# Cross-attention heads on one core: which maximum tiles stand beside which score chunk

## What is computed

```
q = _qdq(x) @ _qdq(wq).T + bq
kv = cond @ wkv.T + bkv
k, v = jnp.split(kv, 2, axis=-1)
...
attn = jax.nn.softmax(jnp.einsum('bnhd,bmhd->bhnm', q, k) * scale, axis=-1)
o = jnp.einsum('bhnm,bmhd->bnhd', attn, v).reshape(B, N, C)
out = _qdq(o) @ _qdq(wp).T + bp
```

## Time and profile before

| | |
|---|---|
| median of 3 runs | 620.76 us |
| profiled execution, its own time | 621.35 us |
| its span (first to last instruction) | 619.5 us |
| mean granted TensorE clock over the span | 0.989 of full |
| busy: PE, PEld | 594.8, 472.6 us |
| busy: DVE, ACT, POOL | 387.1, 305.4, 226.6 us |
| maximum tiles (line 1321), DVE's reads of them (line 982) | 240 of each |
| DMA of keys for the heads (`k_stack`) | 90 of 256 KB |

### The profile page before, as it was taken

How to read it: one execution, slowest core, us unless ns; L and a number is a source line. 1 busy time by engine, 2 the same in 40 slices (tenths; PEclk the granted TensorE clock), 3 DMA queues, 4 the chain that set the end, 5 groups by cost and what they waited for, 6 DMA issues and landing times. The chain is left out here.

```text
span 619.5 us, 12268 instructions
## 1 busy us (share of the span) xinstructions
PE 594.8 (96%) x4264; PEld 472.6 (76%) x4264; DVE 387.1 (62%) x699; ACT 305.4 (49%) x440; POOL 226.6 (37%) x111
## 2 busy tenths in 40 slices
PE   8989999999999999999999999978799899999997
PEld 7867788888887676666666766655698789799996
DVE  3996531430344898988998989956754244376562
ACT  4544233233233665666655666653248668644441
POOL 0000200000011887888888888860001554400000
PEclk9999999999999999999999999987999899999999
DMA  8873655524549666655666666500041324155410
GB/s 300 297 234 129 183 187 161 203 70 164 205 122 288 151 167 167 165 148 148 151 174 164 166 171 160 144 2 2 1 145 59 136 78 195 69 180 195 173 63 35
DMA packets 29758, 92.19 MB, mean 149 GB/s; under 512 B 5472, under 2 KB 9568, under 8 KB 23008
## 3 DMA queue, kind: packets, MB, share of 16 engines
q1 hardware_dynamic: 28480, 89.67, 48.0%
q10 hardware_dynamic: 1248, 2.10, 0.9%
HBM read 65.02 MB, written 18.35 MB: 135 GB/s over the span
## 5 line engine op out<-in xcount | busy, mean ns | idle before, releaser
L982 DVE TENSOR_REDUCE m_part<-ps 128x1 f32<-128x512 f32 x240 | 152.6, 683 | 18.9 <-PE ps L1321 18.3
L716 ACT ACTIVATE p_ring<-ps 128x1024 f32<-128x1024 f32 x128 | 125.6, 1023 | 68.7 <-PE ps L1431 32.6
L589 POOL TENSOR_TENSOR p_sum<-p_sum,p_ring 128x1024 f32<-128x1024 f32 x45 | 107.1, 2380 | 4.1
L1321 PE MATMUL ps<-k_stack,q_max 96*128 96x512 f32 x240 | 92.3, 432 | 0.5 <-issue 0.3
L1419 PEld LDWEIGHTS ps<-q_stack,k_stack 98*128 98x128 f32 x512 | 77.2, 193 | 12.5 <-ACT p_ring L716 4.1
L1419 PE MATMUL ps<-q_stack,k_stack 98*128 98x256 f32 x512 | 85.3, 291 | 0.0
L1431 PE MATMUL ps<-p_ring,v_head 128*32 128x256 f32 x1024 | 70.1, 389 | 1.9 <-ACT o_t L698 1.7
L1321 PEld LDWEIGHTS ps<-k_stack,q_max 96*128 96x128 f32 x240 | 42.3, 188 | 24.5 <-issue 13.8
L937 DVE SCALAR_TENSOR_TENSOR kl_buf<-ps,biases,kh_buf 128x512 fp32r<-128x512 f32 x32 | 23.6, 747 | 55.9 <-ACT kh_buf L670 55.5
L315 DVE TENSOR_TENSOR l_ring<-f_ring,h_ring 128x2048 fp32r<-128x2048 f32 x22 | 50.2, 2287 | 12.5 <-ACT h_ring L311 12.5
L343 PE MATMUL ps<-xt_h,h_ring 128*128 128x256 f32 x200 | 56.8, 284 | 0.0
(11 more groups left out here) (194 smaller groups left out, 1070.5 us busy)
## 6 DMA issues: line engine op xcount, KB each, us to landing
f_ring<-stream SPq DMA_DIRECT2D x29, 1024.0 KB, 4.9
k_stack<-kh_scratch SPq DMA_DIRECT2D x60, 256.0 KB, 4.5
kh_scratch<-kh_buf SPq DMA_DIRECT2D x32, 256.0 KB, 5.6
kl_scratch<-kl_buf SPq DMA_DIRECT2D x32, 256.0 KB, 5.8
v_head<-v_all SPq DMA_DIRECT2D x16, 512.0 KB, 4.0
k_stack<-kl_scratch SPq DMA_DIRECT2D x30, 256.0 KB, 4.1
v_all<-stream SPq DMA_DIRECT2D x4, 256.0 KB, 4.9
f_ring<-stream SPq DMA_DIRECT2D x4, 256.0 KB, 5.5
```

The costliest lines, as they stand in the source:

```text
L589: nc.gpsimd.tensor_tensor(p_sum[:, p, :], p_ring[:, 0, :] if n == 0 else p_sum[:, p, :], p_pair[:] if c == 3 else p_ring[:, c % 4, :], ALU ...
L716: nc.scalar.activation(p_ring[:, c % 4, :], ps[:, 2 * (c % 2):2 * (c % 2) + 2, :].rearrange("p b n -> p (b n)"), ACT.Exp, scale=XSCALE).th ...
L982: nc.vector.reduce_max(m_part[:, j // NT, j % NT:j % NT + 1], maximum_bank(j), AX.X).then_inc(max_read, 1)
L1321: nc.tensor.matmul(maximum_bank(j), q_max[p][0:SPLIT_ROWS, at128(j % NT)], k_stack[p][0:SPLIT_ROWS, j // NT * D:(j // NT + 1) * D], start= ...
```

## The change

Every head keeps its 8 score chunks, 8 value chunks, 16 tiles, merge and rows. What moves is their order on PE, and on DVE the place of the pair sum and of one tile read:

```diff
             negate_maximum(0)
-            chunk_maxima(1, 0, 3)
+            chunk_maxima(1, 0, 4)
...
                 first = isinstance(h, int) and h == 0
-                chunk_maxima(h + 1, 3, 11)
+                chunk_maxima(h + 1, 4, 12)
                 add_pair(h)
-                chunk_maxima(h + 1, 11, 16)
+                chunk_maxima(h + 1, 12, 16)
                 negate_maximum(h + 1)
                 if after:
                     chunk_maxima(h + 2, 0, 1)
                 if not first:
                     normalize_output(h - 1)
                 if after:
-                    chunk_maxima(h + 2, 1, 3)
+                    chunk_maxima(h + 2, 1, 4)
...
                 score(0)
-                next_maxima(3, 5)
+                next_maxima(4, 5)
                 score(1)
                 next_maxima(5, 7)
                 score(2)
-                next_maxima(7, 8)
+                next_maxima(7, 9)
                 score(3)
-                next_maxima(8, 10)
+                next_maxima(9, 10)
                 if not first:
                     summed_denominators(h - 1, 1 - p)
-                next_maxima(10, 11)
+                next_maxima(10, 12)
                 score(4)
-                next_maxima(11, 12)
+                next_maxima(12, 13)
                 score(5)
-                next_maxima(12, 14)
+                next_maxima(13, 15)
                 for c in range(4):
                     value(c)
-                next_maxima(14, 15)
-                score(6)
                 next_maxima(15, 16)
                 if after_loads is not None:
                     maxima(h + 2, p, after_loads, 0, 1)
-                score(7)
+                score(6)
                 if not first:
                     merge(h - 1)
+                score(7)
                 if after_loads is not None:
                     maxima(h + 2, p, after_loads, 1, 2)
                 for c in range(4, 7):
                     value(c)
                 maximum_rows(h + 1)
                 value(7)
                 if after_loads is not None:
-                    maxima(h + 2, p, after_loads, 2, 3)
+                    maxima(h + 2, p, after_loads, 2, 4)
...
             maximum_rows(0)
             pe.wait_ge(ones_set, 3)
-            maxima(1, 1, 1, 2, 3)
+            maxima(1, 1, 1, 2, 4)
             head(0, 0, 1, 1, 2, first=True)
```

## The result

The changed kernel takes 632.88 us (median of 4 runs, 631.56 to 634.4) against 621.68 us of the kernel before in the same comparison. The ratio is 1.018, with a 95% interval of 1.0138 to 1.0221: slower by 1.4 to 2.2%. The profiled execution took 631.56 us, its span is 629.8 us.

A forecast was written before the change was run, and what follows sets the result against it. Prediction: PE is gated at tile 0 by the landing of the keys; 0.25 + 0.48 less about 0.03 us over 14 heads, 9.8, plus 0.6 in head 15, gives 10.4 us: 631.2 us against the median, range 628.0 to 635.0.

The forecast's parts named there:

- The gate: Tile 0 of the head after next waits for its first half of keys, starting 0.24 and 0.22 us after landing.
- Step 1: Moved tiles 3 and 8 put one more tile ahead of score chunk 3, delaying the key load 0.25 us a head.
- Step 2: Score chunk 6 moves from ahead of tile 0 to behind it, costing 0.48 us a head.
- the slack: Slack that early key landings leave at tile 0: about 0.03 us less loss a head.
- Step 3: Merge moved between score chunks 6 and 7, behind tile 0 before and after: no cost.
- Step 4: DVE's pair sum one read later, so POOL's chain ends 0.6 us later; PE waits 0.6 us once, in head 15.
- The sum: Heads 0 to 13 lose 0.70 us each, 9.8 us; with head 15's 0.6 us, 10.4 us in all.
- The keys are not the gate: Tile 0 does not wait for its keys, so the change is not slower: 620.6 us, or 620.0 against the median; 7%.
- The tile 8 rival: Second half of the keys also gates tile 8: 2.1 us more over 14 heads, 633.3 us; 11%.
- The pairs pay: Tiles in pairs and the moved merge remove PE's short waits: at most 5.6 us faster, 615.2 us; 3%.
- The clock: PE's wait in each head lowers the granted clock to 1.2 GHz for 3 us: 21 us more, 652 us; 2%.

The follow-up runs named there:

- run 1: Changed kernel with the first half of the keys loaded as two quarters, each requested earlier: 620.02 us, ratio 0.9995 against the kernel before.
- run 2: Kernel before with the first half of the keys loaded as two quarters, each requested earlier: 619.0 us, ratio 0.9963.
- run 6: Kernel before with the first half of the keys requested after score chunk 4, not chunk 3: 665.76 us in a single run.
- run 3: Changed kernel with score chunk 6 again ahead of tile 0: 626.28 us, ratio 1.0081 against the kernel before.
- the tiles alone: Changed kernel with score chunk 6 ahead of tile 0 and the merge behind chunk 7, as before: 624.68 us, ratio 1.0064 against the kernel before.
- run 4: Kernel before with score chunk 6 alone moved behind tile 0: 626.15 us, ratio 1.0083.
- merge alone: Kernel before with only the merge moved between score chunks 6 and 7: 621.67 us, ratio 1.0020.
- run 5: Two kernels: the change's moved tiles and pair sum only, 624.68 us, ratio 1.0064; kernel before with only the merge moved, 621.67 us, ratio 1.0020.
- the second kernel of run 7: Changed kernel with early key quarters, pair sum back after tile 10's read, and tile 14 back behind the values: 620.38 us, ratio 0.9998 against the kernel before.
- Run 7: Changed kernel with early key quarters and DVE's pair sum back after tile 10's read: 635.7 us, ratio 1.0241; then tile 14 behind the values: 620.38 us.

## Why the prediction was right, by its own steps

- **The gate.** Right, and shown: with earlier keys both orders run at 14.1 us a head (runs 1, 2), with later ones the head grows by nearly the delay (run 6, heads at full clock: 1.8 to 2.1 us for 2.05).
- **Step 1, one tile more ahead of the request,** 0.25 us a head: 0.24 measured in run 3 and in the SP rows of head 6; 0.16 in the tiles alone without their one odd head.
- **Step 2, chunk 6 behind the gate,** 0.48 us less the slack: 0.45 measured (run 4).
- **Step 3, the merge:** nothing, as forecast (merge alone); beside the moved tiles it isn't settled (run 5).
- **Step 4, POOL's chain,** 0.6 us in head 15: the wait grew by 0.62 us, a closer match than the step deserves. From head 14's first scores POOL's end moved by 0.83 us (16.89 to 17.72); run 1 and the second kernel of run 7, which differ in the places of the pair and of tile 14, give 0.82. The mechanism is right and its size was too small, for a reason left open. 0.22 us of it went into head 14, which became that much longer, and the rest is the wait. Nor did it reach the total. The part from head 15's first scores to its merge became 0.59 us shorter, since the clock, low there in both kernels, came back sooner in this execution (6.8 us at the lower level, 10.2 before); further on it was lower for longer (0.66 in the stretch from 445 to 450 us, 1.00 before). These are single executions, and I can't tell which part of that -0.59 and of the +1.23 behind it belongs to the change.
- **The sum.** 9.8 us were forecast for heads 0 to 13 and 9.76 measured: 0.73 a head in heads 1 to 12 and 0.66 in head 13 for a forecast of 0.70, and 0.40 in head 0. For the profiled execution 631.75 was forecast, and it took 631.56. That these meet within 0.2 us is luck, since the parts that nobody forecast (-0.40 ahead of head 0, -0.59 where +0.6 was expected, +1.23 at the end) happen to cancel. The median of the first comparison is 632.88, inside 628 to 635.
- **The rivals.** "The keys are not the gate" falls with run 1. The tile 8 rival came true once, in head 14 (+0.22 us), and elsewhere in this kernel missed by little, at most 0.17 us of idle time. It was underrated: the prediction let landings scatter by 0.1 to 0.2 us, while its own rows go from 4.5 to 4.9, and in run 1, the tiles alone and the second kernel of run 7 a single late second half made one head 0.3 to 1.1 us longer. "The pairs pay" falls: even with the gate removed the change's order (14.12 us) is no faster than the one before (14.11). The Trainium skill, "Perfetto Trace Analysis", section "Matmuls", asks that independent groups rotate through PSUM banks; both orders rotate their tiles through the same three, so the prediction was wrong to say that this rule prefers the change. The clock did not fall in the heads of the changed kernel.

What the prediction left out is why the pair sum moves at all. It priced the move as a small loss at the end. Run 7 shows that without it tile 14, ahead of the values, costs over 1 us a head once the keys come early. With the keys loaded as in the change this was not run, and part of that time might lie beside the wait for them.

## What to carry to other kernels

When a double buffer is refilled in the middle of its own last use, the way from the request to the first consumer of the new data (issue, landing) is the same in every order. Count the work ahead of the request and the work behind the consumer, since both lengthen the loop. Work moved from in front of such a consumer to behind it costs nearly its full time (0.45 us of 0.48 in run 4), even when PE looks busy all along. Before rearranging work around the wait, ask for the data in pieces, each as soon as its own last reader is done; here that gave 0.86 us a head in the changed order and 0.14 in the order before. Then look at the next wait on the same buffer: it was the second half's that showed up.

## What the runs showed of the hardware that was not expected

- The profile's name for what ended a wait at tile 0 differed between rows of one tile (DVE's read in the weight loads' row, the DMA in PE's). The distance to the landing, 0.23 to 0.30 us in every head of the loop in both kernels, was the surer sign.
- The last of three 256 KB DMAs landed 4.0 to 5.7 us after its issue in the traces of the two kernels, mostly 4.5 to 4.9, and once 6.3 in the tiles alone; the last of three 128 KB ones, first quarters in run 1, took 2.6 to 4.3.
- In run 6 a wait of 1.58 us was followed by a fall of the granted clock, and one of 1.93 us in another head was not.
